# First cross attention of a decoder: the exponentials, transposes and products with V run one step later, with six weight buffers

## What the reference computes

```
attn = einsum('bhqd,bhkd->bhqk', q, k) * scale
attn = softmax(clip(attn, -CLAMP, CLAMP))            # CLAMP = 10000
attn = where(any(isnan(attn)), 1.0 / Nkv, attn)      # over the whole tensor
x    = einsum('bhqk,bhkd->bqhd', attn, v) @ Wo + bo
```

## Time and profile before

| what | value |
|---|---|
| three runs | 1881.14, 1899.2 (median), 1905.21 us |
| the profiled execution: its own time | 1887.83 us |
| the profiled execution: its span | 1886.0 us |
| X0, first to last maximum of a step (DVE, L357) | 650.69 to 849.14 us |
| S1, first to last maximum | 1218.24 to 1364.79 us |
| X1, first to last maximum | 1411.38 to 1572.94 us |
| busy over the span | PE 68%, DVE 59%, ACT 41%, POOL 45% |
| mean granted TensorE clock | 0.794 of full |

### The profile page before, as it was taken

The page is one execution under the profiler, slowest core; times in us unless marked ns, Lnnn a source line. Parts: engine busy times, 40 slices in busy tenths (PEclk is TensorE's granted clock), DMA queues, the critical chain, the costliest instruction groups (busy, mean ns, idle before and its releaser), DMA issues. The chain is left out here.

```text
span 1886.0 us, 27391 instructions
## 1 busy us (share of the span) xinstructions
PE 1285.3 (68%) x9658; PEld 838.4 (44%) x9658; DVE 1112.4 (59%) x2432; ACT 773.6 (41%) x1360; POOL 842.1 (45%) x618
## 2 busy tenths in 40 slices
PE   5678777777767368883214996399859996224992
PEld 2233233233223146563214996166636665224882
DVE  2899989989997357653431111577625763442335
ACT  3544545544532155551002553276625772002331
POOL 2666666666673267771662554110010110564552
PEclk8798898898998578875556998599956996556996
DMA  4102102102100510003115775500030001115675
GB/s 157 69 23 96 68 28 96 69 28 96 69 28 6 121 18 2 2 2 96 38 43 170 228 226 163 130 7 19 13 98 1 19 13 50 50 42 172 212 214 165
DMA packets 106652, 148.38 MB, mean 79 GB/s; under 512 B 14029, under 2 KB 82938, under 8 KB 102228
## 3 DMA queue, kind: packets, MB, share of 16 engines
q1 hardware_dynamic: 95220, 128.94, 22.7%
q0 software_dynamic: 9088, 17.07, 2.6%
q10 hardware_dynamic: 2208, 0.61, 0.1%
HBM read 113.96 MB, written 34.45 MB: 79 GB/s over the span
## 5 line engine op out<-in xcount | busy, mean ns | idle before, releaser
L889 POOL TENSOR_TENSOR M_dbx<-M_u,M_b_sb 128x1024 f32<-128x1024 f32 x128 | 300.0, 2355 | 128.9 <-DVE M_h L976 127.6
L976 DVE TENSOR_TENSOR_SCAN M_h<-M_pA,M_dbx 128x512 f32<-128x512 f32 x256 | 310.8, 1214 | 6.0 <-POOL M_dbx L889 5.0
L1127 ACT ACTIVATE M_pA<-M_dt,M_a_neg 128x504 f32<-128x504 f32 x256 | 173.8, 683 | 277.4 <-DVE M_h L976 276.5
L1244 PE MATMUL M_pY<-M_hc,M_ident 128*128 128x512 f32 x512 | 279.4, 675 | 6.3 <-DVE M_y_sum L994 6.3
L1499 POOL DMA_INDIRECT F_answers<-F_yblk,F_xblk x156 | 151.5, 971 | 159.5 <-DVE F_yblk L1627 118.0
L986 DVE TENSOR_TENSOR M_hc<-M_h,M_pC 128x512 f32<-128x512 f32 x256 | 169.4, 662 | 35.9 <-issue 23.3
L1492 POOL DMA_INDIRECT F_slots<-F_line,F_pos x128 | 125.4, 979 | 68.3 <-issue 48.0
L1755 PE MATMUL F_bank<-F_xT,F_wbuf 128*128 128x256 f32 x624 | 153.9, 391 | 0.9 <-ACT F_xT L1670 0.9
L1244 PEld LDWEIGHTS M_pY<-M_hc,M_ident 128*128 128x128 f32 x512 | 108.9, 214 | 94.1 <-issue 81.2
L1232 PE MATMUL M_pC<-M_split,M_sel_bf 96*128 96x512 bf16 x128 | 53.9, 421 | 133.2 <-DVE M_hc L986 132.9
L357 DVE TENSOR_REDUCE X_smax<-X_pS 128x8 f32<-128x512 f32 x128 | 82.4, 685 | 99.6 <-PE X_pS L598 99.6
(11 more groups left out here) (260 smaller groups left out, 2304.6 us busy)
## 6 DMA issues: line engine op xcount, KB each, us to landing
M_b_sb<-M_rows_bc SPq DMA_DIRECT2D x32, 1024.0 KB
F_wbuf<-in_F_wcat SPq DMA_DIRECT2D x39, 578.0 KB
F_wbuf<-in_F_wcat SPq DMA_DIRECT2D x39, 450.0 KB
F_xblk<-F_slots SPq DMA_DIRECT2D x78, 132.0 KB
F_ya<-F_answers SPq DMA_DIRECT2D x16, 512.0 KB, 7.0
x<-X_x SPq DMA_DIRECT2D x16, 256.0 KB
X_kv<-in_ctxT SPq DMA_DIRECT2D x2, 1344.0 KB, 10.1
F_answers<-F_yblk,F_xblk POOLq DMA_INDIRECT x156
```

The lines of the kernel that those rows point to most:

```text
L889: pool.tensor_tensor(dbx[:, k % DBXS, :, :], u[:, g % 2, :, :], bc(b_sb[:, n, :], 1, 2), ALU.mult).then_inc(dbx_ready, 1)
L976: v.tensor_tensor_scan(h[:, k % STATES, half, :], pA[:, (2 * k + half) % DECAYS, :, :].rearrange("p b t -> p (b t)"), dbx[:, k % DBXS, hal ...
L1127: act.activation(pA[:, (2 * k + half) % DECAYS, :, 1:SEQ], dt[:, g % 2, half, :].rearrange("p (b t) -> p b t", t=SEQ)[:, :, 1:SEQ], ACT.Ex ...
L1244: ins = pe.matmul(pY[:, half, :], ident[:, :], hc[:, k % HCS, half, :], start=(n == 0), stop=(n == N - 1))
```

## The change

Guarded form only (X0): LAG is 1 there and 0 in S1 and X1, whose instruction lists keep their order. s_sb has 6 slots in place of 4 in X0. On ACT, exponent and copy_pt, and on PE, transposes and products with V, go one step later in the list (e = i - 1 in place of i), and so does normalise on DVE; the loops have one step more. Scores, maxima, the subtraction and POOL's minimum stay at step i. add_bias(c) moves from group c to group c + 1, the last one behind the loop. The setup of the NaN case moves from ahead of the loop into its first three steps, on DVE behind the subtraction of steps 0, 1 and 2, on PE at the end of steps 0 and 1; PE waits for alt_ready only ahead of its first product with V.

```
+    LAG = 1 if guarded else 0
+    SLOTS = 4 + 2 * LAG
...
-        s_sb = m.sb("s_sb", [P, 4, GROUP])
+        s_sb = m.sb("s_sb", [P, SLOTS, GROUP])
...
-                if s == 0:
+                if s == 0 and not guarded:
                     add_bias(c)
+                if s == 0 and guarded and c >= 1:
+                    add_bias(c - 1)
...
+            if guarded:
+                add_bias(GROUPS - 1)
...
             def less_max(n):
-                reach(v, pt_psum, n - 3)
+                reach(v, pt_psum, n - SLOTS + 1)
...
-            for i in range(STEPS + 2):
+            for i in range(STEPS + 2 + LAG):
...
                     less_max(2 * i)
                     less_max(2 * i + 1)
-                if i >= 3 and i % 2 == 1:
-                    normalise((i - 3) // 2)
+                if guarded and i == 0:
+                    mean_of_context()
+                if guarded and i == 1:
+                    mean_of_v()
+                if guarded and i == 2:
+                    other_rows()
+                if i >= 3 + LAG and (i - LAG) % 2 == 1:
+                    normalise((i - LAG - 3) // 2)
...
-            for i in range(STEPS + 1):
+            for i in range(STEPS + 1 + LAG):
                 c, s = i // PER, i % PER
-                if i >= 1:
-                    copy_pt(2 * i - 2)
-                if i < STEPS:
-                    exponent(2 * i)
+                e = i - LAG
+                if e >= 1:
+                    copy_pt(2 * e - 2)
+                if 0 <= e < STEPS:
+                    exponent(2 * e)
...
                 if i < STEPS:
                     scores(i)
-                if i >= 2:
-                    weights_times_v(2 * i - 4)
-                    weights_times_v(2 * i - 3)
-                if 1 <= i <= STEPS:
-                    turn_weights(2 * i - 2)
+                if e >= 2:
+                    if guarded and e == 2:
+                        pe.wait_ge(alt_ready, 1)
+                    weights_times_v(2 * e - 4)
+                    weights_times_v(2 * e - 3)
+                if 1 <= e <= STEPS:
+                    turn_weights(2 * e - 2)
...
+                if guarded and i == 0:
+                    pe.wait_ge(guard, 1)
+                    pe.matmul(pO[:, P:P + BATCH], wv_all[:, :], kv_mean[:, :], start=True, stop=True
+                              ).then_inc(alt_psum, 1)
+                if guarded and i == 1:
+                    pe.wait_ge(guard, 2)
+                    pe.matmul(pO[0:BATCH, 2 * P:3 * P], v_mean[:, :], wo[:, :], start=True, stop=True
+                              ).then_inc(alt_psum, 1)
```

More of the change, by code:

```diff
@@ L317, in not_over_zero @@
                 pool.wait_ge(s_used, n + 1)
-                pool.tensor_scalar(s_sb[:, n % 4, :], s_sb[:, n % 4, :], 0.0, None, ALU.min).then_inc(s_low, 1)
+                pool.tensor_scalar(s_sb[:, n % SLOTS, :], s_sb[:, n % SLOTS, :], 0.0, None, ALU.min).then_inc(s_low, 1)
             rstd(0)
@@ L366, in less_max @@
             def less_max(n):
-                reach(v, pt_psum, n - 3)
+                reach(v, pt_psum, n - SLOTS + 1)
                 s = pS[:, n % 4, :].rearrange("p (h k) -> p h k", k=KEYS)
-                out = s_sb[:, n % 4, :].rearrange("p (h k) -> p h k", k=KEYS)
+                out = s_sb[:, n % SLOTS, :].rearrange("p (h k) -> p h k", k=KEYS)
                 if guarded:
@@ L407, in _, with mean_of_context @@
             v.tensor_tensor(bias[:, :], pO[:, 0:D], bo[:, :], ALU.add).then_inc(bias_ready, 1)
-            if guarded:
+            def mean_of_context():
                 v.wait_ge(kv_first, 16)
@@ L412, in _, with mean_of_v, other_rows @@
                 v.tensor_scalar(kv_mean[:, :], kv_mean[:, :], 1.0 / KEYS, None, ALU.mult).then_inc(guard, 1)
+            def mean_of_v():
                 v.wait_ge(alt_psum, 1)
                 v.tensor_scalar(v_mean[:, :], pO[:, P:P + BATCH], bv_col[:, 0:1], None, ALU.add).then_inc(guard, 1)
+            def other_rows():
                 v.wait_ge(alt_psum, 2)
                 v.tensor_tensor(alt_rows[:, :], pO[0:BATCH, 2 * P:3 * P], bo[0:BATCH, :], ALU.add).then_inc(alt_ready, 1)
-            for i in range(STEPS + 2):
+            for i in range(STEPS + 2 + LAG):
                 c, s = i // PER, i % PER
@@ L506, in exponent @@
                 act.wait_ge(s_low if guarded else s_used, n + 1)
-                act.activation(s_sb[:, n % 4, :], s_sb[:, n % 4, :], ACT.Exp).then_inc(exp_done, 1)
+                act.activation(s_sb[:, n % SLOTS, :], s_sb[:, n % SLOTS, :], ACT.Exp).then_inc(exp_done, 1)
             def copy_pt(n):
@@ L535, in _ @@
                     copy_oT(c - 1)
[L536 to L539, removed]
+                if e >= 1:
+                    copy_pt(2 * e - 1)
+                if 0 <= e < STEPS:
+                    exponent(2 * e + 1)
                 if c + 1 < GROUPS:
@@ L606, in turn_weights @@
                 for k in range(4):
-                    ins = pe.transpose(pPT[:, k * P:(k + 1) * P], s_sb[:, n % 4, k * P:(k + 1) * P], ident[:, :])
+                    ins = pe.transpose(pPT[:, k * P:(k + 1) * P], s_sb[:, n % SLOTS, k * P:(k + 1) * P], ident[:, :])
                 ins.then_inc(pt_psum, 1)
@@ L678, in _ @@
                     turn_o(c - 1)
-                if 1 <= i <= STEPS:
-                    turn_weights(2 * i - 1)
+                if 1 <= e <= STEPS:
+                    turn_weights(2 * e - 1)
                 if s == 0 and c >= 2:
```

## The result

The changed kernel takes 1830.6 us (median of 4, 1821.1 to 1833.6), the kernel before 1893.6 (1881.1 to 1905.2): a ratio of 0.968, 95% interval 0.964 to 0.972. That is 63 us less where 38 were forecast, and under the stated range. Three later comparisons, each on another chip, gave 0.966, 0.968 and 0.963.

The account below looks back on a forecast made before the run. The prediction took POOL's and DVE's latency inside X0's PE-ACT round trip as the bound. Its terms, -29 + 0.5 - 13.5 + 4 = -38 us, taken from 1893.5, gave 1855 us, with a range of 1836 to 1880.

Parts of the forecast that it names:

- What bounds the kernel: X0: no engine is full; DVE's and POOL's latency lies inside the PE-ACT round trip, groups taking 23.98 us against X1's 19.25.
- Term 1: X0, steps 8 to 31: the lag brings X1's pace, 113.0 us in place of 142.1, so -29 us (-31 to -15).
- rival in which the change gets slower: X0, steps 8 to 31: PE waits longer in list order and never regains the clock; +17 us, 1911, chance 0.05.
- Term 2: X0, NaN setup up to step 1's maximum: the mean is moved, not hidden; +0.5 us, up to 2 us above it.
- Term 3: X0, steps 1 to 8: alt is awaited later, step 8's maximum at 694 in place of 707.03; -13.5 us (-16.5 to -5.5).
- Term 4: X0, the end: one more step of products and transposes behind the last scores; +4 us (2 to 5.5).
- -46 to -26: X0: the stated reach of the forecast's terms in us, around their sum of -38.
- low-clock rival: X0: PE falls back to its low clock for a fifth of steps 8 to 31, so 1873 us; chance 0.17.
- port rival: X0, DVE: every limit waits for POOL, DVE becomes the bound at 21.2 us a group, so 1864; chance 0.12 with POOL's lateness.
- the minimum lets the limit through: X0, DVE: a pair of limits took 0.30 us inside POOL's minimum, only POOL's additions held it up (1.25 us).
- slack: X0, POOL ahead of ACT's exponential: lateness of 2.2 us against a slack of 2.5, fitting narrowly.

Follow-up runs that it names:

- before_filled4: The kernel before with four useless 128x128 products added on PE in each step of X0; ratio 0.986 to the kernel before.
- early_mean: The changed kernel with the context mean taken ahead of DVE's second layer norm and PE's first product of it ahead of the loop; ratio 0.962 to the kernel before.
- after_d: The changed kernel, nothing altered, profiled again on another chip; ratio 0.963 to the kernel before, X0 184.0 us.
- before_b: The kernel before, nothing altered, profiled a second time; X0 245.0 us, a group 27.40 us.
- pool_more: The changed kernel with two more additions of 1.27 us on POOL in each group of X0; one run, X0 183.4 us, a group 19.70 us.
- before_c: The kernel before, nothing altered, profiled a third time; X0 243.8 us, a group 27.40 us.

## Why the prediction was wrong, point by point

**What bounds the kernel: right.** The loop through POOL was the cause, the lag removed it, and X1's pace was the pace after.

**Term 1 (steps 8 to 31, forecast -29): mis-sized, and the failed step.** It was -32.8 in the pair of profiles (142.1 to 109.3) and -46 and -45 from the two later profiles of before (155.5 and 154.4). Two errors. I took 113.0 from X1, part of whose steps ran at the low level, and the lower bound of 110.7 was the better value. Much larger: I took 142.1 as what X0 costs. It was one profile, and the fastest of three. In that profile X1 took 161.6 us from first to last maximum and S1 146.5, which showed that phases with nearly the same lists can differ by 15 us in one execution; I used the clock for a rival in which the change gets slower, and put at nothing what the low clock was costing the kernel before: some 10 us of the 142.1 by before_filled4, and 22 to 23 in the two later profiles.

**Term 2 (+0.5): right**, +0.3 (12.35 us behind the bias and not 12.08). The setup's 6.9 us were moved, not hidden; PE waited 6.3 us for the mean. early_mean shows the place where they are hidden.

**Term 3 (steps 1 to 8, -13.5): mechanism right, size short.** 53.4 to 36.5, -16.9. POOL waited 2.7 us for alt, at 676.9 (forecast 3 to 8 us, near 680). The clock first reached its high level by step 3 (1.00 from 663 to 666 us), some 2 us earlier than I allowed, and fell once more (0.53 from 669 to 672). From the later profiles of before (59.6 and 59.4 us) the same term is -23.

**Term 4 (+4): right at equal clock, absent in the pair.** With the clock at 0.50 the end takes 22.6 us (after_d) where before_b takes 17.9, so +4.7. In the pair it took 16.1 us at a clock of 0.94 against 16.5 at 0.60, so the later step and the better clock cancel: -0.4.

**Where the 25 us are.** The sum in the pair of profiles was -49.8 and not -38: 3.8 from term 1, 3.4 from term 3, 4.4 from term 4 and 0.2 from term 2. Other phases of the pair gave another 4.5, and 8.7 lie between the pair (-54.3) and the medians (-63.0). No single execution shows these 13; that X0 of before took 20 us more in both later profiles would more than cover them, but that the timed executions did the same is argued, not shown.

**Range and chances.** The range allowed 46 us and 11 more for the spread. The "-46 to -26" given as the reach of the terms doesn't follow from their own bounds, whose upper ends add up to about -13. The low-clock rival had the sign wrong: closing gaps raises the clock. The port rival is out: groups took 19.25 us with DVE busy for 17.96. My reading that the minimum lets the limit through was too simple, though. Of the 23 pairs of limits from step 8 to 30, ten took under 0.3 us, one 1.25, and twelve 0.53 to 0.73, most of them beside POOL's minimum, as here:

```profile
732.92 0.53 DVE L369 TENSOR_SCALAR X_smax<-X_smax 128x8 f32<-128x8 f32 x2
```

From step 8 to 31 the limits kept DVE busy for 12.0 us in all, against 13.8 in the kernel before, so this cost nothing here. The slack was as narrow as I said, 0.6 us at s = 1. Running over it costs mostly what POOL's time costs, and once, in pool_more, a stretch at the low clock with it.

## What to carry to other kernels

An engine's latency inside another engine's round trip is priced by a sibling phase that runs without it; such a yardstick gave the pace after to 0.1%. Where PE's clock moves, the cost of a gap can be the gap and the low clock behind it, so a change that closes gaps can be worth more than the gaps. Before a sum is made from one profile, phases with nearly the same lists in it should be compared: if they differ, the phase to be changed may have had a fast or a slow course too, and a second profile, or at least that spread in the range, is due.

## What was not expected of the hardware

Two to four useless 128x128 products per step in PE's waiting time made the kernel before 1.2 and 1.4% faster, as the granted clock went from 0.72 to 0.81 in the profiles of before up to 0.90 and 0.98. And chips differ outside this phase: the kernel before took 1840 and 1841 us on two of them and 1886 to 1894 on three others, with X0 the same (245.0 in before_b, 243.8 in before_c) and the stretch behind X1 266.3 and not 301.8 us.
